# Four zero fills of a preparation stage move from SyncE's instruction stream to ScalarE's

## The reference

```python
xn = _layernorm(x, axis=-1)
x = x + _L0_attn_ref(xn, ...) + _L0_ffn_ref(xn, ...)
...
norm_q = rmsnorm(x @ W_cq, q_scale)          # q from a 128-wide latent
norm_kv = rmsnorm(x @ W_ckv, kv_scale)       # k, v from a 64-wide latent
...
attn = jax.nn.softmax(scores, axis=-1)       # causal, 16 heads, 512 x 512 per batch
out = jnp.einsum('bhqk,bhkd->bhqd', attn, value) ... @ W_o
...
topk_w, topk_i = jax.lax.top_k(scores, TOP_K)
routed = jnp.einsum('tef,efd,te->td', act, wd, combine)
shared = jax.nn.silu(hidden_states @ sg) * (hidden_states @ su) @ sd
```

## Time and profile before

| what | value |
|---|---|
| median of the runs (lowest, highest) | 1461.12 us (1458.72, 1465.09) |
| profiled execution, first to last instruction (its span) | 1463.6 us |
| mean clock granted to PE over the span | 0.969 of full |
| PE busy / DVE / ACT / POOL | 1301.1 / 939.1 / 852.3 / 589.6 us |
| preparation, until DVE's first work in the next block | 30.76 us |
| one batch of `project` (third to fifth) | 16.17 us |

### The profile page before, as it was taken

One profiled execution on the slowest core, in us unless ns is written; L12 is line 12 of the kernel. 1 busy time (PEld: TensorE's weight loads), 2 busy tenths in 40 slices (PEclk: granted clock), 3 DMA queues, 4 the chain that ended last, 5 costly groups with the idle time before them and its releaser, 6 DMA issues. The chain is left out here.

```text
span 1463.6 us, 24454 instructions
## 1 busy us (share of the span) xinstructions
PE 1301.1 (89%) x7385; PEld 962.3 (66%) x7385; DVE 939.1 (64%) x3726; ACT 852.3 (58%) x2294; POOL 589.6 (40%) x607
## 2 busy tenths in 40 slices
PE   4899769999999999539999999997898998998996
PEld 3566446777776677328888888885566665665664
DVE  3587777777777777102565323335879888788884
ACT  1455347677666766216556666665666666666663
POOL 1111037677677777200000000003666566666663
PEclk8899989999999999859999999998999999999999
DMA  9777652323335222285965555542232332332321
GB/s 351 297 253 270 231 194 94 105 80 109 106 141 186 91 87 77 94 257 174 345 190 179 177 178 177 175 152 65 87 105 81 107 101 81 106 109 81 98 77 60
DMA packets 132179, 216.98 MB, mean 148 GB/s; under 512 B 14486, under 2 KB 108374, under 8 KB 126806
## 3 DMA queue, kind: packets, MB, share of 16 engines
q1 hardware_dynamic: 99798, 152.48, 30.7%
q0 software_dynamic: 18432, 50.36, 10.9%
q10 hardware_dynamic: 13824, 12.59, 2.8%
HBM read 103.70 MB, written 111.67 MB: 147 GB/s over the span
## 5 line engine op out<-in xcount | busy, mean ns | idle before, releaser
L1633 ACT ACTIVATE l_prob<-l_prob,l_negmax 128x512 f32<-128x512 f32 (+3 forms) x256 | 142.1, 556 | 152.7 <-DVE l_negmax L1719 129.3
L989 POOL DMA_INDIRECT sorted_x<-f_xn_row,slot_no x192 | 205.0, 1068 | 49.7 <-issue 48.8
L1145 ACT ACTIVATE f_prob<-f_prob,f_negmax 128x512 f32<-128x512 f32 (+3 forms) x256 | 142.6, 557 | 119.5 <-DVE f_negmax L1218 110.6
L1526 PE MATMUL ps<-l_kt,l_qt 128*128 128x512 f32 (+3 forms) x512 | 176.2, 451 | 39.8 <-DVE l_qt L1697 22.9
L2061 DVE TENSOR_TENSOR act_f<-hidden,ps 128x96 f32<-128x96 f32 x224 | 57.0, 254 | 239.4 <-ACT hidden L2036 239.0
L1464 POOL DMA_INDIRECT l_rows<-sorted_y,slot_no x192 | 185.8, 968 | 49.1 <-issue 41.1
L1996 PE MATMUL ps<-wgu_sb,xt_e 128*128 x896 | 186.1, 331 | 20.4 <-DMA wgu_sb<-in_wgu 17.9
L1048 PE MATMUL ps<-kt_s,f_qt 128*128 128x512 f32 (+3 forms) x512 | 170.4, 446 | 7.2 <-DVE f_qt L1209 4.4
L1218 DVE CUSTOM_DVE_ANT_0 f_prob<-ps,mask_add 128x512 f32<-128x512 f32 (+3 forms) x256 | 121.0, 486 | 80.4 <-issue 79.4
L1719 DVE CUSTOM_DVE_ANT_0 l_prob<-ps,mask_add 128x512 f32<-128x512 f32 (+3 forms) x256 | 121.9, 485 | 72.4 <-issue 71.2
L1492 POOL MEMSET l_one<- 128x1 f32 x1 | 0.1, 99 | 389.2 <-POOLq L1922 389.2
(11 more groups left out here) (201 smaller groups left out, 2936.8 us busy)
## 6 DMA issues: line engine op xcount, KB each, us to landing
sorted_x<-zeros SPq DMA_DIRECT2D x14, 2048.0 KB, 9.3
rows_in<-sorted_x SPq DMA_DIRECT2D x112, 256.0 KB, 2.9
sorted_y<-rows_out SPq DMA_DIRECT2D x112, 256.0 KB, 2.1
wgu_sb<-in_wgu SPq DMA_DIRECT2D x4, 1536.0 KB, 12.9
x_in<-in_x SPq DMA_DIRECT2D x8, 512.0 KB, 10.0
xn_dram<-xn SPq DMA_DIRECT2D x8, 512.0 KB, 3.8
base_dram<-x_in SPq DMA_DIRECT2D x8, 512.0 KB, 2.9
nqt_dram<-nqt_out SPq DMA_DIRECT2D x8, 512.0 KB, 3.9
```

Source lines behind the costliest of these rows:

```text
L989: pool.indirect_dma_start(sorted_x, bass.IndirectOffsetOnAxis(ap=slot_no[:, t, k:k + 1], axis=0), xn_row[buf][:], None).then_inc(scattered ...
L1145: act.activation(prob[:, i, qt, 0:w], prob[:, i, qt, 0:w], ACT.Exp, bias=negmax[:, i, qt:qt + 1], scale=-1.0, accum_out=rowsum[:, g // 2 % ...
L1526: mm = pe.matmul(s_ps[k % 2][:, 0:w], qt[g // 2 % 2][g % 2][:, n * P:w], kt[b - HB][:, 0:w], start=True, stop=True)
L1633: act.activation(prob[:, i, qt, 0:w], prob[:, i, qt, 0:w], ACT.Exp, bias=negmax[:, i, qt:qt + 1], scale=-1.0, accum_out=rowsum[:, g // 2 % ...
```

## The change

The four fills of the preparation leave SP's stream, where they stood behind the loads of x, and stand in ACT's stream behind its last work of the block, the copy into `rope_t`. The wait for the tile of zeros moves along. Sizes, addresses and the semaphore that they raise stay the same.

```diff
@@ -198,10 +198,6 @@
                 sp.dma_start(tile_c[:], tile_no).then_inc(loaded, 16)
                 for i in range(XBUF):
                     sp.dma_start(x_in[i][:], x_t[i]).then_inc(x_loaded[i], 16)
-                sp.wait_ge(zeros_made, 1)
-                for i in range(EARLY):
-                    sp.dma_start(zero_part[i], zeros[:].unsqueeze(1).to_broadcast([P, zero_part.shape[2], ZCOLS]))\
-                        .then_inc(zeros_stored, 16)
                 sp.wait_ge(loaded, 10 * 16)
                 sp.wait_ge(table_loaded, 16)
 
@@ -253,6 +249,11 @@
                 split(None, act, wvo_s[0][:], None, wvo_ps, prep_hi, 0, None)
                 act.wait_ge(table_turned, 1)
                 act.activation(rope_t[:], table_ps, ACT.Copy)
+
+                act.wait_ge(zeros_made, 1)
+                for i in range(EARLY):
+                    act.dma_start(zero_part[i], zeros[:].unsqueeze(1).to_broadcast([P, zero_part.shape[2], ZCOLS]))\
+                        .then_inc(zeros_stored, 16)
```

## The result

The changed kernel took 1469.72 us (median of 20 runs, 1463.47 to 1476.49), the kernel before 1466.97 us in as many runs. The ratio is 1.0029, 95% interval 1.0016 to 1.0043: slower by 0.29%, some 4.2 us (2.3 to 6.3). The two medians alone differ by 2.75 us, which lies in that interval. The span of the profiled execution went from 1463.6 to 1465.0 us.

A forecast was written before the change was run, and what follows sets the result against it. PE's order of work was taken to bound the kernel, with no batch of `project` catching up on a delay. Removed 0 and added 3.8 us on the median: 1461.1 + 3.8 = 1464.9 us, range 1458 to 1471.

The forecast's parts named there:

- Faster or slower by over 0.5%, 7.3 us, is about what a measurement of this kernel can tell from no change: Whole kernel: smallest difference taken as measurable, since three runs alone spread over 6.4 us.
- same: Whole kernel: outcome neither faster nor slower by over 0.5%, chance 0.82; slower had 0.14, faster 0.04.
- the sum: First batch of `project`: removed 0, added 3.8 us; the barrier's 2.2 disappear inside that and 1.16 are not won.
- Ten idle microseconds of DVE are worth 1.16 us to PE: First batch: DVE waits 10.50 us for the store of `xn`, but the delay costs PE only 1.16 us.
- The barrier's delay is hidden under the store's: Before `project`: ACT's issues open the barrier 2.2 us later, which disappears inside the store's 3.8 us.
- Piece for piece: First store of `xn` beside the fills: one small piece per 8 KB piece, 10.9 us for the store's 512.
- Rival A: First batch: the store overtakes the fills and DVE's stall is gone, +1.0 us, 1462.1; chance 0.15.
- Then both simply end together, at 50.5 plus the store's own 1.3 us = 51.8: First batch: the store ends with the fills, so DVE starts at 52.5 instead of 48.61, +3.9 us.
- Rival B: First batch: PE's clock falls in the longer pause, 3.8 + 4.6 = +8.4 us, 1469.5; chance 0.12.
- My point of decision: First batch: a PE pause of two microseconds can be enough for its clock to fall.
- The price of 4.6: First batch: the remaining 6.7 us of PE work would take 4.6 us more at half clock.
- Rival C: Before `project`: ACT is blocked in its issues, the barrier opens at 37.2, +5.6 us, 1466.7; chance 0.04.

The follow-up runs named there:

- e1: Kernel before with the four early fills issued later, in `heads_first`, so none stands near the first store of `xn`: 1485.03 us in one run (before 1464.70).
- e2: Changed kernel with ACT's four transfers cut to 256-byte pieces, real fills issued in `heads_first`: 1486.27 us in one run (before 1464.70).
- e3: Changed kernel with ACT's four issues moved behind the barrier, first in its `project` stream: 1468.72 us in one run (before 1464.70).
- e11: Changed kernel run once more, nothing altered: 1475.96 us in a single execution (before 1467.13).
- e4: Changed kernel with six fills on ACT instead of four (`EARLY = 6`): 1480.41 us in one run (before 1464.70).
- the repeats: Kernel before and changed kernel, each run once more unaltered: 1463.93 and 1475.96 us (before 1467.13 beside them).
- e8: Same kernel as e3, ACT's four issues first in `project` behind the barrier, now timed: ratio to before 1.0034 (1.0019 to 1.0050).
- e9: Changed kernel with ACT's four issues ahead of the copy into `rope_t` instead of behind it: ratio to before 1.0001 (0.9989 to 1.0012).
- e7: Kernel before with two fills kept in the preparation and two issued by SP behind the first store of `xn`: ratio 0.9987 (0.9970 to 1.0005).
- e5: Changed kernel with ACT's four fills cut into 512 pieces of 4 KB instead of 256 of 8 KB: 1471.79 us in one run (before 1467.28).

## Why the prediction was right and where it was wrong

The size and the sign came out: 3.8 us slower forecast, 4.2 (2.3 to 6.3) measured, and 0.29% lies within the 0.5%. The step that failed is the last one, "Faster or slower by over 0.5%, 7.3 us, is about what a measurement of this kernel can tell from no change". I took that from the spread of three runs, and put 0.82 on "same"; 20 runs of each kernel tell 0.29% apart, with an interval of some 0.13% to either side. The trace argued for slower, and the text should have said so first. In the sum the mechanism held, but one term was too small: the second `xn` came 5.9 us later after the copy's start, where the sum added 3.8. That the runs' 4.2 lies nearer to 3.8 is in part luck; their interval holds both. And the time of 1464.9 stood on the low median of three runs: 1469.72 is 4.8 us above it, but only the difference to the kernel before in as many runs tests the forecast.

- **Ten idle microseconds of DVE are worth 1.16 us to PE**: right. e1 removed them all and won 1.5.
- **The barrier's delay is hidden under the store's**: right in the main. In e2, without the load, the delay comes out; in e3, without the delay, the cost stays. Its size was off: the issues took 4.10 us (4.09 in e11), not 3.19, above even my upper bound of 3.85, so the delay was 3.5 instead of 2.2. By the sum, in which the store lands with the end of the fills, that does not matter; no run isolates it.
- **Piece for piece**: right, 328 to 316 and 453 to 447. The Trainium skill's turn of a whole packet of 9 to 17 descriptors ("DMA: Bandwidth & Descriptors", "Queues, rings and completion order") would have let the store's small pieces through in groups; no run shows that, and on the one engine that still works from 51.5 the two queues' pieces alternate singly. Rival A, which rested on it, fell. The 10.9 us for the store's 512 pieces were a little short, 12.2 in e4; the forecast did not hang on them.
- **"Then both simply end together, at 50.5 plus the store's own 1.3 us = 51.8"**: this is the term that was mis-sized. From an actual start of the fills near 29.8 it gives 51.0, so landing at 51.7. It landed at 53.6. I had divided the work evenly among the engines. The window from 52 to 54, with 0.04 of the engines' time busy, and the records of the pieces show one engine finishing alone from 51.5 to 53.2, 1.7 of the missing 1.9 us, and the store landed only behind its last piece. In e11 one engine also finishes alone, for 1.7 us; why it lags stays open. From the copy's start the second batch begins 5.9 us later (6.8 in the repeats) instead of 3.8.
- **Rival B, the clock**: not in the profiled execution (1.00 throughout, with a pause of 3.19 us), but in the repeat, behind a pause of 2.75 us, and in all three executions with pauses above five (e3, e4, e8). My point of decision, two microseconds, did not part the cases: 2.75 us and 3.19 came out the other way round. The price of 4.6 was too high: only part of the batch's products runs at 1.2 GHz, 1.7 us in e11.
- **Rival C**: no issue blocked ACT for long; all four together took 4.10 us.
- **The end.** The delay is 5.03 us at the next block's first fills (192.16 before, 197.19 after), as every batch takes the same. Behind that the single executions drift apart: at the experts' first load it is only 1.8 us. These are the first fills of the changed kernel, and then the experts' first load in the kernel before and in the changed one:

```profile
197.19 1.20 SPq L945 DMA_DIRECT2D sorted_x<-zeros  x2
```

```profile
613.76 0.24 SPq L1946 DMA_DIRECT2D expert_row<-tile_expert  x1
```

```profile
615.56 0.24 SPq L1947 DMA_DIRECT2D expert_row<-tile_expert  x1
```

In the repeats the same row stands at 611.99 and 622.44. One difference is seen: before has a window at half clock there (0.62 from 600 to 604), after has 1.00 from 604 to 606. How much of the rest is clock and how much transfers stays open. So the difference of the two spans, 1.4 us, is not the cost; the ratio of the runs is, and it agrees with the trace up to 197.

## What to carry to other kernels

When a transfer is moved to another engine, ask first when it now starts: e9, e8 and the changed kernel use the same engine and queue, and only e9, whose issues come earlier, is not 0.3% slower. Here a bulk write beside a store of small pieces cost the store as much as one ahead of it (12.8 us to landing in e9, 12.3 before). So put the bulk where the DMA engines idle and what doesn't fit behind the store, as e7 does; its stretch is 1.2 us shorter than before's, though the whole kernel was not told apart from no change. And an idle engine's wait is worth only what the bound engine waits for it: here 1.5 of 10 us.

## What the runs showed of the hardware

- Handing over four transfers of 256 pieces on ACT took 4.10 us with 8 KB pieces and idle DMA engines, 2.58 with 256 bytes, and 2.62 with 8 KB behind loads still running (e9).
- A store of 512 pieces of 1 KB beside a continuous stream of 8 KB pieces took 17.1 to 17.3 us to land in three executions (e3, e4, e8), against 3.8 for the usual one. Its first piece moved 4.2 to 4.3 us after the issue, and its 512 pieces then took 12.2 to 12.4.
- The two queues moved piece for piece whether the fills' pieces were of 8 KB (328 to 316, changed kernel) or of 4 KB (464 to 467, e5).
- In the first batch PE's clock fell to 1.2 GHz in or behind pauses of 2.75 to 5.6 us in four executions (e3, e4, e8, e11), and held at 2.4 GHz through one of 3.19 (changed kernel).
